# A four-layer decoder kernel on one core: the order of its 2338 steps as a list in the source, in place of a list scheduler

## The reference, cut to what matters

```python
x = _layernorm(x + _L0_attn_ref(x, ...))             # L0a: causal attention, 16 heads of 8, rotary with scale
x = _layernorm(x + _L0_xattn_ref(x, ctx, ctx, ...))  # L0x: cross attention to 154 keys
x = _layernorm(x + _L0_ffn_ref(x, ...))              # ffn0: quantised linear, depthwise conv, silu, linear
x = _layernorm(x + _L1_attn_ref(x, ...))             # heads1: attention over the 16 heads of one position
x = _layernorm(x + _L1_xattn_ref(x, ctx, ctx, mask, ...))  # L1x
x = _layernorm(x + _L1_ffn_ref(x, ...))              # moe1: 16 experts, top 2, with a capacity
x = _layernorm(x + _L2_attn_ref(x, ...))             # L2a: causal attention, rotary
x = _layernorm(x + _L2_xattn_ref(ctx, x, ctx, mask, ...))  # L2x
x = _layernorm(x + _L2_ffn_ref(x, ...))              # ffn2: gated silu, two gelu layers of 512
x = _layernorm(x + _L3_attn_ref(x, ...))             # self3: one head of 128 with a distance bias
x = _layernorm(x + _L3_xattn_ref(x, ctx, ctx, ...))  # L3x
x = _layernorm(x + _L3_ffn_ref(x, ...))              # moe3: 8 experts, routing weights
```

## Time and profile before

| | |
|---|---|
| runs | 1827.08, 1827.16 and 1831.81 us, median 1827.16 |
| the profiled execution | 1836.74 us, its span 1835.0 us |
| busy in the span | PE 1396.8 us (76%), DVE 1115.1 (61%), ACT 707.1 (39%), POOL 360.2 (20%) |
| instructions | PE 9530, DVE 2336, ACT 1012, POOL 427 |
| granted TensorE clock, mean | 0.85 of full speed |

### The profile page before, as it was taken

The page is one execution under the profiler, slowest core; times in us unless marked ns, Lnnn a source line. Parts: engine busy times, 40 slices in busy tenths (PEclk is TensorE's granted clock), DMA queues, the critical chain, the costliest instruction groups (busy, mean ns, idle before and its releaser), DMA issues.

```text
span 1835.0 us, 25733 instructions
## 1 busy us (share of the span) xinstructions
PE 1396.8 (76%) x9530; PEld 663.7 (36%) x9530; DVE 1115.1 (61%) x2336; ACT 707.1 (39%) x1012; POOL 360.2 (20%) x427
## 2 busy tenths in 40 slices
PE   3678878755545675785668989888799799977886
PEld 1333323321322331442234535334344344444443
DVE  3677747786686578579866546654225424257745
ACT  0245556632423123112524452445525335433342
POOL 3224540023114105204421030111301200020000
PEclk7669988865766886896788989999899899988897
DMA  7702132000100310512031141120301501041111
...
DMA packets 50072, 86.35 MB, mean 47 GB/s; under 512 B 13718, under 2 KB 42198, under 8 KB 45526
## 3 DMA queue, kind: packets, MB, share of 16 engines
q1 hardware_dynamic: 49950, 84.71, 20.0%
...
## 4 chain that ended last, share of the span: by engine, by line
PE 51%; DVE 23%; ACT 8%; DMA 6%; issue 6%; SPq 5%; POOL 2%; ACTq 0%; POOLq 0%; DVEq 0%
PE ps L1032 6%; PE ps L1186 6%; PE ps L1152 5%; PE ps L959 4%; PE ps L1153 4%; DVE MX L1396 4%; PE ps L1159 3%; PE ps L870 3%; ACT WORK L1818 3%; PE ps L965 3%; SPq L2157 2%; DVE SIDE L1530 2%; PE ps L917 2%; DVE SIDE L1534 2%; PE ps L1081 2%
## 5 line engine op out<-in xcount | busy, mean ns | idle before, releaser
L1396 DVE TENSOR_REDUCE MX<-ps 128x3 f32<-128x462 f32 (+5 forms) x704 | 412.2, 628 | 217.3 <-PE ps L965 151.3
L1818 ACT ACTIVATE WORK<-ps 128x1024 f32<-128x1024 f32 (+1 forms) x352 | 312.3, 947 | 137.1 <-PE ps L993 92.2
L959 PE MATMUL ps<-KH,QH 48*128 48x154 bf16 (+5 forms) x1536 | 145.8, 279 | 129.9 <-DVE MX L1396 77.0
L1032 PE MATMUL ps<-WORK,VA 128*18 128x512 f32 (+3 forms) x1536 | 171.5, 542 | 4.1 <-ACT WORK L1818 3.5
L2068 POOL TENSOR_TENSOR SIDE<-SIDE 128x2048 f32<-128x2048 f32 x16 | 101.7, 6355 | 369.4 <-ACT SIDE L1887 328.1
L959 PEld LDWEIGHTS ps<-KH,QH 48*128 48x128 bf16 (+1 forms) x1536 | 61.2, 100 | 294.2 <-DVE MX L1396 153.7
L1912 ACT ACTIVATE SIDE<-ps 128x512 f32<-128x512 f32 x96 | 57.2, 597 | 273.9 <-PE ps L1153 273.7
L993 PE MATMUL ps<-QH,KH 54*128 54x512 bf16 (+3 forms) x768 | 122.2, 372 | 51.1 <-ACT WORK L1818 35.6
L2058 POOL TENSOR_SCALAR_AFFINE_SELECT WORK<-WORK 128x256 f32<-128x256 f32 (+1 forms) x192 | 95.1, 500 | 307.7 <-ACT WORK L1818 307.4
L1642 DVE TENSOR_TENSOR SIDE<-SIDE,ps 128x512 f32<-128x512 f32 x96 | 65.9, 688 | 120.7 <-ACT SIDE L1912 120.7
L1159 PE MATMUL ps<-SIDE 128*128 128x128 f32 x768 | 107.3, 285 | 36.6 <-DVE SIDE L1653 19.7
...
## 6 DMA issues: line engine op xcount, KB each, us to landing
...
```

What stands on the lines that cost most here:

```text
L959: mms[b] = pe.matmul(banks[b][:, c * pitch:c * pitch + width], qr[b][:, h, t * 128:t * 128 + 128], kr[b][:, h, 0:width], start=(c == 0), s ...
L1032: mm = pe.matmul(ps[32 * j:32 * j + 2 * NV, UB, q0:S], lhsT.rearrange("p a c -> p (a c)"), PB[:, (PAIR_BASE[F] + where[pi]) % NSLOT, b, at ...
L1396: dve.tensor_reduce(MX[:, 32 * b + i0:32 * b + i0 + cnt], src, AX.X, ALU.max, negate=True).then_inc(freed, 1)
L1818: act.activation(PB[:, N % NSLOT, :, lo:hi], wide_banks("pair", F, n)[:, :, lo:hi], ACT.Exp).then_inc(sem("exp_done"), 1)
```

## The change

`plan()`, its costs and its bonuses go. Three short lists give the order of the attention stages, of the stages that share the tile SIDE, and of the tails; `STEPS` gives the kinds of all steps in order, and `ordered_items()` deals each kind's steps out in the order of the stages. The three stage orders are those that `plan()` made. The multiset of steps, and what each step issues on each engine, is the same. Ahead of a third and fourth `h0t` of a batch the second-last `h0b` is now asked for in the list, which adds no instruction. What changes is the order of steps of different stages among each other, nearly everywhere; line numbers of the engines' code fall by 136.

```diff
@@
-def plan():
-
-    todo = {}
-    for stage in CHAIN:
-        for b in range(B):
-            todo.update(stage_items(stage, b))
...
-    return fronts, out
-
-
-FRONTS_KEYS, ITEMS = plan()
+FRONT_ORDER = """
+L0a.0 L0a.1 L0a.2 L0a.3 L0x.0 L0x.1 L0x.2 L0x.3 L1x.0 L1x.1 L2a.0 L1x.2 L2a.1 L1x.3 L2x.0 L2x.1 L2a.2 L2a.3 L2x.2 L2x.3
+L3x.0 L3x.1 L3x.2 L3x.3
+""".split()
...
+STEPS = """
+project*5 base pieces project send project*4 max*5 pieces max*9 send max*8 split project*2 max turn max project max pair
...
+def ordered_items():
+
+    waiting = {kind: [(kind, ("setup", 0), 0)] for kind in ("base", "rest", "masks", "w0", "tables2")}
+    tail = ("wo", "square", "mean", "x")
+    for key in keys(FRONT_ORDER) + keys(SIDE_ORDER):
+        for kind, _, i in stage_items(*key):
+            if kind not in tail:
+                waiting.setdefault(kind, []).append((kind, key, i))
+    for kind in tail:
+        waiting[kind] = [(kind, key, 0) for key in keys(TAIL_ORDER)]
+    out = []
+    for step in STEPS:
+        kind, _, times = step.partition("*")
+        for _ in range(int(times or 1)):
+            out.append(waiting[kind].pop(0))
+            if kind == "max":
+                out.append((kind, out[-1][1], out[-1][2] + 1))
+    assert not any(waiting.values()), waiting
+    return out
+
+
+FRONTS_KEYS, ITEMS = keys(FRONT_ORDER), ordered_items()
@@ in stage_items, ffn0
-            add("h0t", q, [("silu0", FC - 1)], [("h0t", q - 1)] if q else [])
+            add("h0t", q, [("silu0", FC - 1)], ([("h0t", q - 1)] if q else []) + ([("h0b", q - 2)] if q >= 2 else []))
```

More of the change, by code:

```diff
@@ L142 @@
 EXPERTS = {"moe1": NE, "moe3": NE3}
[L143 to L148, removed]
[3 rows of a table removed]
-          "pair": 4.7, "wide": -54.4}
@@ L153 @@
[L153 to L206, removed]
[6 rows of a table removed]
[L213 to L217, removed]
@@ new lines @@
+pair max copy project out project pair max out project*2 pair value*2 pieces pair mix pair value pair send w0 copy split
+wo turn out pair max value square pair max pair mean max value x max value project copy project out project*2 max mix
+pair max wo max pair*2 max value square max mean max pair x pair max value pieces split send pair q0x pair value copy
+pair*2 max q0t pair max h0 turn max h0 value*3 copy pair max silu0*3 out value silu0 out pair max h0t*2 mix pair h0b
+pair max h0t wo h0b h0t square mean h0b*2 pair max x wo pair*2 q0x square value max pair*2 value q0t pair copy max h0
@@ new lines @@
+mean h0 value out silu0 value*2 silu0 copy max out silu0*2 h0t mix h0t h0b h0t h0b h0t h0b wo x h0b square wo max split
+qkv mean qkv hs turn hv hs hm pair*2 qkv square value pair*2 hv value pair hs value hm qkv pair copy out pair mean
+pair*2 tables2 pair value*2 hv hs hm value copy out mix x wo square mean hv hm x ht q0x wo q0t x square h0 mean x h0
+project silu0*4 project*3 pieces send h0t*2 h0b h0t h0b h0t h0b*2 max wo max q0x square max q0t max h0*2 silu0 max
+silu0*3 max*2 h0t*2 h0b h0t h0b h0t h0b mean max*2 x h0b max wo max split qkv*2 turn pair hs hv pair square qkv mean
@@ new lines @@
+project*2 dn project ew project dn gu max ew gu pair max dn value max pair ew*2 max dn ew pair max gu max gu project
+dn*2 max copy split gu value pieces send ew*2 max dn out gu ew max value dn turn gu*2 dn ew value max ew dn copy gu max
+ew gu dn out dn gu max ew mix gu dn wo square dn pair max ew*2 gu max gu mean value max pair max pair max dn*2 pair max
+pair max acc pair x max wo square max pair max value max pair max value wide max pair max mean w3 x g2*2 project*4 max
+g2 copy max project pieces g2 pair max hid2 split hid2 send out turn hid2 max value pair max value max pair*2 max value
@@ new lines @@
+max pair*2 copy hid2 pair max value max pair value max value pair max out pair*2 max value max pair*2 value max value
+pair max pair mix pair wide max value*2 copy max pair wo max pair*2 square value max pair value max pair value pair*2
+max out value max pair*2 value max value*3 max copy mean out x hid2 split turn hid2*2 pair*2 mix hid2 pair*2 wo*2 pair
+square pair value square value pair*2 mean value wide value pair x pair project pair value pair*2 project g2*2 value*3
+project copy project pieces g2*2 send mean pair out hid2*2 pair max value wide pair max pair*2 max value max pair value
@@ new lines @@
+pair*2 max pair hid2 pair*2 max x value max value*2 max hid2 max value*2 copy max hid2 out hid2 mix max wo hid2 split
+square hid2 mean x turn wo project*2 f3 pair project*2 s3 square s3 value fk3 pieces pt3*2 mean pt3*2 pair send max wo
+max pair*2 square max pair max x value max mean f3 x pair max pair max value project s3 copy project max s3 fk3 max pair
+max pair*2 max value*2 pt3*3 split value pt3 project copy project pieces send out turn out wo square mix pair*2 max wo
+square mean value x max mean x pair max pair project max pair*2 max wide pair value max pair*2 max value max pair max
@@ new lines @@
+copy g2 project g2 value max project g2 project g2 value*2 max out pieces copy hid2*3 split hid2 out send wide turn hid2
+mix hid2 max pair wo square hid2*2 mean wo max pair*2 square x max pair wide value max pair*2 max pair value max pair
+value max copy pair*2 max value max g2*2 max value g2*2 wide max value split copy out hid2*2 out hid2 mix hid2 mean hid2
+x hid2 turn hid2*2 wo square wo pair square pair f3 mean x s3*2 value fk3 pt3 pair pt3*3 mean wo square pair x pair
+value f3 mean s3 x s3 project value project copy pair fk3 pt3*4 project pair*2 wo project out square pieces log mean
@@ new lines, with keys @@
+dn pair*2 dn ew value*2 pair gu*2 value x dn out copy ew*2 dn gu out gu mix dn wo square ew dn gu ew gu mean dn*2 x acc
+log ew*2 top ew gu*2 wo square dn*2 ew gu*2 dn*2 ew gu ew gu dn ew*2 fin dn gu*2 dn*2 mean acc wo fin square mean x fin
+x fin
+""".split()
+def keys(names):
+    return [(name.split(".")[0], int(name.split(".")[1])) for name in names]
+def ordered_items():
[16 more added lines that the diff above has]
+    return out
@@ L596, in check_plan @@
 def check_plan():
+    at = {item: n for n, item in enumerate(ITEMS)}
+    for stage in CHAIN:
+        for b in range(B):
+            for item, (data, order) in stage_items(stage, b).items():
+                for needed in data + order:
+                    assert at[needed] < at[item], (needed, item)
     where = {it: n for n, it in enumerate(PLAN)}
```

207 lines of the change are left out of this document (46 added, 161 removed), and 9 rows, old and new, of tables (URGENT, costs).

## The result

| | before | after |
|---|---|---|
| median of the runs (range) | 1829.49 us (1827.08 to 1833.68) | 1756.1 us (1754.31 to 1756.74) |
| ratio to before, 95% interval | | 0.9595 (0.9572 to 0.9618) |
| span of the profiled run | 1835.0 us | 1752.6 us |

The account below looks back on a forecast made before the run. The kernel was taken as bound by latency between engines over long parts. From the profiled 1836.74 us, -27.7 (stops), -21 (short waits) and +10 (table loads) gave 1798.0, or 1788 us in a timed run; range 1748 to 1834.

Parts of the forecast that it names:

- the first rival: Whole kernel: short waits go in full (42 us) and a higher clock gives 13, so 1754 us; chance 0.22.
- the likeliest case: Whole kernel: 1788 us in a timed run, 2.1% less, with 1775 to 1802 us given chance 0.37.
- Stops at sends: Six stops of PE and DVE together, 30.5 us in all: better cover removes 27.7 us; ends 0 and 30.5.
- Short waits: PE's waits for a single partner, ACT or DVE: about 42 us can go, half taken, 21 us; ends 0 and 42.
- The five waits: PE hands a bank to ACT or DVE: `copy`-`out`, `out`-`mix`, `square`-`mean` and two in the experts, 84.6 us in all.
- Clock: PE from 350 to 1000 us: in the first rival, mean clock 0.80 instead of 0.75 gives 13 us on the path.
- Table loads: ACT: 24 more loads of 1.283 us, 30.8 us of work, taken to cost 10 us.
- The rival in which ACT becomes the bound: From moe1.2 to L2x, new loads hold back silus, exponentials and PE, 53.5 us: slower, 1853 us; chance 0.13.
- the 1863 us: ACT-bound case priced by the skill's 2.66 us a switch: 24 switches add 63.8 us against 27.7 gained.
- Alternation: PE turns between forms of matmul 26 times more often: at most 6.5 us, taken as 0.
- the five places: First `pair` of L2a.1, first maxima of L1x.1, L2x.2, L3x.0, L3x.2: no PE and DVE stop over 3 us.
- sign of error: New stops at L0x.2, L2x.3 or L2a.2 summing to more than 15 us would show the prediction wrong.

Follow-up runs that it names:

- e3: The kernel before with only its six stops mended, by moving a load and first maxima; 1827.25 us, ratio 0.9972.
- e4: The kernel after, with the first maxima of fourteen fronts moved behind independent steps that fill their stop; 1753.49 us, ratio 0.9581.
- e11: e9 plus nine of the fourteen moves of e4 (fronts L0x.0 to L2x.0); 1743.53 us, ratio 0.9529.
- e9: The kernel after with one step moved: `rest` stands behind the split of L0a.0, as in before; 1745.3 us, ratio 0.9532.
- e10: The kernel before, with the next `gu` put ahead of `dn` at 28 places where PE waits for DVE; 1831.98 us, ratio 1.0005.
- e5: The kernel before, with next independent PE steps put ahead at 89 of PE's waits for DVE or ACT; 1880.99 us, ratio 1.0296.
- e6: The kernel after, with the same edit as e5 at 75 waits of 72.8 us; 1819.92 us, ratio 0.995.
- e12: The kernel before, with only the 139 steps behind the mean of L1x.0 up to `x` of L1x.1 in the new order; 1811.27 us, ratio 0.989.
- e2: The new order up to `x` of L1x.3 (1434 steps), then the order of before; 1805.02 us, ratio 0.9852.
- e7: The kernel before with Identity in place of silu and gelu, so 26 table loads go; 1830.67 us, ratio 1.0008.
- e8: The kernel after with Identity in place of silu and gelu, so 39 table loads go; 1752.02 us, ratio 0.9578.

## Why the prediction was right, and where it was not

The sign and the range are right, and so is the ground for them: both engines wait for each other over long parts, and another order of the same steps shortens these waits. The size that came, 1756, is that of the first rival, "more than that" (1754), not the 1788 of the likeliest case. That the rival's sum comes within 2 us is luck: two of its terms, -27.7 and +10, did not happen, and the waits and the clock gave more than it took for them.

**Stops at sends, -27.7: failed, in both its halves.** First, the covers were summed for the six fronts that stop in before and for three more, not for all 24. The stops of L2a.1, L2x.2 and L3x.0 went as said. L1x.1 still has 5.8 us and L2x.1 4.7. L3x.2, which was to go as a whole, became longer: PE waits 11.4 us for its keys where it waited 3.0, and DVE stops with it for 4.4. New ones stand at L2a.0 (8.6), L2a.2 (6.9), L2a.3 (6.4), L2x.0 (5.6), L1x.0 (5.3), L1x.3 (5.0), L0x.1 (4.6), L2x.3 (3.1) and L0x.2 (3.0). PE's waits for DMA rose by 38.5 us. Second, a stop was priced by its length. In e3, e4 and e11 the time in which PE and DVE both stop for over 1.2 us shrank by 18, 30 and 15 us, for gains of 5, 3 and 1 us, none clear of its interval and none above 12. Part of the steps pulled ahead waited themselves, for weights or maxima from the same queue; where a stop did go, waits for DVE and ACT grew elsewhere.

**The stop that nobody saw.** At 104 us ACT's 13 us of `rest` hold up PE and DVE (10.7 us). The order shows `rest` behind `pieces` of L0a.2 there, and I had not looked at ACT in the head. It costs 11 us, about its length (e9).

**Short waits, -21: the term that was mis-sized.** The five waits of the earlier trace rows went from 84.6 to 50.8 us (15.5 + 6.2 + 14.9 + 13.1 + 1.1), 33.8 less, near the 42 that I counted and halved. What I left out was larger: `pair` waiting for ACT's exponential (L857, 35.6 to 11.1) and `turn` for the split (25.8 to 6.8). All waits of PE for ACT and DVE fell from 338 to 232 us, 106 less. But counting places between partners is no price: e10 empties such waits for nothing, and e5 and e6 make the kernel 3 and 4% slower with an edit that looks like an improvement at each of its places, in e5 in good part by waits that it opened itself. What is shown is that the gain belongs to whole stretches: by e12 20 us to some 140 steps behind L1x.0, by e2 27 to the first 1434, the rest to those behind, and that it appears as shorter waits of PE for DVE and ACT, with both busy together. Which feature of the order within a stretch makes it stays open; no run isolates one. `x` beside POOL (last section) could be up to 4.7 us of the 20 in e12 and 8 of the whole; that is untested.

**Clock, 0 in the sum and 13 in the rival: too small.** PE's busy time fell by 26 us of 82 between the two profiled executions, and by 14 of 79 between e7 and e8 in the same two orders. The sum had nothing for it. In the stretch of e12 it is 10 of 21 in one pair of traces and 2.5 of 17 in the other, so the size of this part is uncertain. That it is above 0 is not: the timed runs have clocks of 0.865 to 0.872 after and 0.846 to 0.863 before.

**Table loads, +10: nothing measurable.** The loads are 77, ACT's busy time is 738.9, as said; of the 24 new ones 13 are ahead of a silu or gelu and 11 at an Exp or Ln, where the prediction had twelve and twelve. e7's interval allows 26 loads to cost at most 2 us and e8 finds 3 us, within both intervals, for 39. The rival in which ACT becomes the bound has nothing left, nor has the 1863 us that the prediction worked out from the Trainium skill's 2.66 us a switch. The waits of PE for L1818 fell from 46.6 to 19.4 us.

**Alternation, 0:** no run separates it.

**What the profile was to show.** Right: table loads, DVE and POOL within 1%, the clock over 0.86, idle time of PE below 438, though 382 instead of 400. Wrong: of the five places L1x.1 has its stop still (5.8 us) and L3x.2 4.4 us in two pieces, and the idle time of 1000 to 1600 us is 53 us instead of under 45. `L734 <-ACT WORK` is 15.5 where half of 22.0 was asked; `<-DVE OK` 6.2, under half of 16.4. The new stops at L0x.2, L2x.3 and L2a.2 sum to 13.0, just under the 15 that I had set as a sign of error; the sign was too narrow, as the stops stood elsewhere.
